# A new order of the units of the second attention, one store of rows a unit, and heads loaded from rows of sixteen

## The reference

```python
dist = softmax(mean(x @ Wr + br, axis=1))          # 16 heads, one row an image
idx = sort(top_k(dist, 4))                         # 4 heads of 16 for each image
Q, K, V = x @ Wq + bq, x @ Wk + bk, x @ Wv + bv    # 16 heads of 64 features
Qs, Ks, Vs = (the four chosen heads of each image)
O = softmax(Qs @ Ks.T / 8) @ Vs                    # 17 x 17 scores
return O.transpose(...) @ Wo + bo                  # then added to x
```

## Time and profile before

| what | value |
|---|---|
| runs | 406.89, 409.97, 404.96 us; median 406.89 |
| profiled execution | 407.69 us, its span 405.9 us |
| busy: PE, weight loads, DVE, ACT, POOL | 317.0, 259.3, 257.0, 202.8, 168.5 us |
| routing ready, first weights issued | 225.4 us from the span's start |
| first `qk` of unit 0, of unit 9 | 230.3 us, 348.8 us |
| last `head_out` begins with its pair at | 370.9 us |
| indirect fetch begins | 377.3 us |

### The profile page before, as it was taken

How to read it: one execution, slowest core, us unless ns; L and a number is a source line. 1 busy time by engine, 2 the same in 40 slices (tenths; PEclk the granted TensorE clock), 3 DMA queues, 4 the chain that set the end, 5 groups by cost and what they waited for, 6 DMA issues and landing times.

```text
span 405.9 us, 15412 instructions
## 1 busy us (share of the span) xinstructions
PE 317.0 (78%) x6584; PEld 259.3 (64%) x6584; DVE 257.0 (63%) x544; ACT 202.8 (50%) x461; POOL 168.5 (42%) x188
## 2 busy tenths in 40 slices
PE   1999999888877778758972598888796887672877
PEld 1896868346755656547852498777786876561366
DVE  2455555635778888875966477767775676633175
ACT  1113342637867666713891347666566565533140
POOL 3853000005366666630550733566644675352300
PEclk9999999999955555556985579999999999987699
DMA  7999100008000000000000678788686776722614
GB/s 205 390 427 405 81 2 0 0 0 289 26 3 6 5 4 5 3 5 2 2 1 0 203 228 266 232 247 242 173 267 170 231 224 177 225 69 48 199 62 184
DMA packets 40225, 53.84 MB, mean 133 GB/s; under 512 B 13244, under 2 KB 36956, under 8 KB 39644
## 3 DMA queue, kind: packets, MB, share of 16 engines
q1 hardware_dynamic: 39068, 50.50, 38.5%
q0 software_dynamic: 576, 2.23, 1.6%
q10 hardware_dynamic: 512, 0.11, 0.2%
HBM read 45.02 MB, written 7.81 MB: 130 GB/s over the span
## 4 chain that ended last, share of the span: by engine, by line
PE 34%; SPq 28%; DVE 12%; issue 11%; ACT 6%; DMA 4%; POOL 4%; POOLq 0%; ACTq 0%; DVEq 0%
SPq L433 17%; PE ps L1291 11%; SPq L422 5%; PE ps L1314 5%; SPq L438 5%; PE ps L1445 4%; POOL r L512 3%; DVE r L984 3%; PE ps L1627 3%; PE ps L1374 3%; PE ps L1396 2%; DVE rs L994 2%; PE ps L1329 2%; DMA r<-in_x 2%; DVE mx L969 2%
## 5 line engine op out<-in xcount | busy, mean ns | idle before, releaser
L505 POOL TENSOR_TENSOR r<-r,cst 128x1088 f32<-128x1088 f32 x16 | 33.0, 2066 | 61.7 <-DVE ring L920 58.9
L1291 PE MATMUL ps<-r 128*128 128x256 f32 x192 | 45.4, 392 | 8.7 <-DMA r<-in_x 8.7
L1291 PEld LDWEIGHTS ps<-r 128*128 128x128 f32 x192 | 37.4, 198 | 15.7 <-issue 10.6
L1396 PE MATMUL ps<-r 17*32 17x34 f32 x2048 | 30.3, 242 | 16.5 <-DVE r L984 11.8
L1396 PEld LDWEIGHTS ps<-r 17*32 17x32 f32 x2048 | 27.3, 142 | 24.3 <-DVE r L984 18.9
L697 ACT ACTIVATE r<-r,cst 128x136 f32<-128x136 f32 x128 | 39.9, 402 | 0.0
L1511 PE MATMUL ps<-r,ring 128*128 128x68 f16 x840 | 37.2, 201 | 1.9 <-issue 1.9
L767 ACT ACTIVATE r<-ps 128x504 f16<-128x504 f32 (+1 forms) x50 | 32.1, 667 | 11.4 <-PE ps L1489 10.8
L1489 PE MATMUL ps<-pairs_of,r 128*128 128x56 f16 x680 | 29.7, 193 | 9.7 <-DVE r L1156 5.8
L588 POOL TENSOR_TENSOR r<-r,quad 128x476 f16<-128x476 f16 x38 | 37.0, 1008 | 0.0
L1509 PE MATMUL ps<-tile_head,wb 128*128 128x68 f16 x140 | 27.8, 199 | 10.2 <-DMA ring<-wsplit 8.3
(11 more groups left out here) (160 smaller groups left out, 752.5 us busy)
## 6 DMA issues: line engine op xcount, KB each, us to landing
ring<-wsplit SPq DMA_DIRECT2D x140, 192.0 KB, 3.2
r<-in_x SPq DMA_DIRECT2D x3, 1536.0 KB, 15.8
r<-in_w SPq DMA_DIRECT2D x4, 768.0 KB, 12.7
wsplit<-ring SPq DMA_DIRECT2D x1, 3072.0 KB, 11.7
padded_rows<-r SPq DMA_DIRECT2D x36, 56.0 KB
r<-in_x SPq DMA_DIRECT2D x4, 384.0 KB, 8.7
h<-in_pos SPq DMA_DIRECT2D x1, 1536.0 KB, 11.9
out<-h SPq DMA_DIRECT2D x3, 512.0 KB, 2.7
```

Source lines behind the costliest of these rows:

```text
L505: pool.tensor_tensor(free(kx[:, u % 2, 0, :], (ROWH, UI), (NTOK, HH), (1, NTOK)), free(kr[:, 0, UI * NTOK * u:], (NTOK, UI), (0, HH), (1, ...
L1291: mm = pe.matmul(bank((n - 1) % 2, 0, D), xT[:, c, k, i * P:(i + 1) * P], tokw[:, k, :], start=k == 0, stop=k == PKT - 1)
L1396: mm = pe.matmul(bank(4 + 2 * (u % 2) + j // 2, at, at + 2 * NTOK)[QROW * c:QROW * c + QROW], v1[rows, UG * u + g, lo:lo + QROW], p1T[rows ...
```

## The change

Four things change together.

**Heads.** `heads` holds a row of 16 numbers for each unit, 14 of them used, so unit v's load begins at byte 64 v.

**Rows.** In `padded_rows` a pair has 32 rows of 256 bytes, not 17. One transfer stores all 128 partitions of a unit's `o2` (1,792 runs of 256 bytes, of which 840 are padding); the last unit has two such, by seven tiles, both on SP. ACT issues none. SP issues the weights of both parts of unit v and then the store of unit v - 3.

**Waits by part.** Where an instruction of part r of unit v waited until both parts of unit v - 2 were read, it waits for part r alone.

**Order.** All four engines get a new order. `weigh2` runs two units behind `qk`, not one, except at the end. `split_weights`, `low_halves` and `soft_out` are cut into their instructions, and these are placed one by one. The last unit has an order of its own on each engine. `gather`, `gathered`, `qk`, `v_of`, `scores2` and `weigh2` themselves are as before.

```diff
+HEADS_UNIT = 16
-PITCH = NTOK * HD2
+PITCH = QROW * HD2
...
-def pair_rows_of(v, j, lo=0, n=GU):
-    return bass.AP(padded_rows.tensor, (v * PU + IPG * lo + j) * PITCH,
...
+def rows_of(v, lo=0, n=GU):
+    return bass.AP(padded_rows.tensor, (v * PU + IPG * lo) * PITCH, [(HD2, P), (IPG * PITCH, n), (1, HD2)])
...
     def heads_of(v):
         _, head = nc.values_load_multi_w_load_instructions(
-            heads[0:1, GU * v:GU * v + GU], engines=(mybir.EngineType.SP,), min_val=0, max_val=NE - 1,
+            heads[0:1, HEADS_UNIT * v:HEADS_UNIT * v + GU], engines=(mybir.EngineType.SP,), min_val=0, max_val=NE - 1,
             skip_runtime_bounds_check_because="the head of a tile, and no more than NE - 1")
         return head
...
-    def store_pairs(v, j):
-        sp.dma_start(pair_rows_of(v, j), o2[QROW * j:QROW * j + NPATCH, v % 2])\
-            .then_inc(o2_stored[v % 2], 16)
-        if j == IPG - 1:
-            sp.dma_start(last_rows_of(v), o2[NPATCH:P:QROW, v % 2]).then_inc(o2_stored[v % 2], 16)
+    def store_rows(v):
+        sp.wait_ge(o2_ready, 2 * (v + 1))
+        sp.dma_start(rows_of(v), o2[:, v % 2]).then_inc(o2_stored[v % 2], 16)
     for v in range(NV):
         head = heads_of(v)
         weights_in(head, 2 * v)
+        weights_in(head, 2 * v + 1)
         if v >= 3:
-            sp.wait_ge(o2_ready, 2 * (v - 2))
-            for j in range(IPG):
-                store_pairs(v - 3, j)
-        weights_in(head, 2 * v + 1)
+            store_rows(v - 3)
     for v in range(NV - 3, NV - 1):
-        sp.wait_ge(o2_ready, 2 * (v + 1))
-        for j in range(IPG):
-            store_pairs(v, j)
-    last = o2[:, (NV - 1) % 2]
+        store_rows(v)
     for lo in (0, GR):
         sp.wait_ge(o2_ready, 2 * (NV - 1) + lo // GR + 1)
-        for j in range(IPG // 2):
-            sp.dma_start(pair_rows_of(NV - 1, j, lo, GR), last[QROW * j:QROW * j + NPATCH, lo:lo + GR])\
-                .then_inc(o2_stored[(NV - 1) % 2], 16)
-        sp.dma_start(last_rows_of(NV - 1, lo, GR), last[NPATCH:P:QROW, lo:lo + GR])\
+        sp.dma_start(rows_of(NV - 1, lo, GR), o2[:, (NV - 1) % 2, lo:lo + GR])\
             .then_inc(o2_stored[(NV - 1) % 2], 16)
...
         if v >= 2:
-            pool.wait_ge(s2_done, 2 * (v - 1))
-        if r == 0 and v == 0:
+            pool.wait_ge(s2_done, 2 * (v - 2) + r + 1)
+        if (v, r) == (0, 0):
             pool.wait_ge(xg_clear, 4)
             pool.wait_ge(bd_clear, 2)
-        elif r == 1 and v >= 1:
-            pool.wait_ge(bd_ready, 4 * v)
-        elif r == 0 and biased(v):
+        elif v <= 1 and (v, r) != (1, 1):
+            pool.wait_ge(k2_twice, 2 * v + r)
+        elif (v, r) == (NV - 1, 1):
+            pool.wait_ge(pT_high, NV - 1)
+        elif r == 1:
+            pool.wait_ge(bd_ready, 4 * (v - 1) + 1)
+        elif biased(v):
             pool.wait_ge(hbo_ready, biased(v))
         else:
-            pool.wait_ge(k2_twice, 2 * v + r)
+            pool.wait_ge(bd_ready, 4 * (v - 1))
...
-    def split_weights(v):
+    def split_high(v):
+        pool.wait_ge(k2_twice, min(2 * v + 3, 2 * NV))
         pool.wait_ge(p2T_ready, v + 1)
-        used = lambda x: free(p2Tx[:, v % 2, x], (QROW, GU), (1, NTOK))
-        full = free(p2T[:, v % 2], (QROW, GU), (1, NTOK))
...
-        pool.tensor_copy(used(0), full).then_inc(pT_high, 1)
+        pool.tensor_copy(free(p2Tx[:, v % 2, 0], (QROW, GU), (1, NTOK)),
+                         free(p2T[:, v % 2], (QROW, GU), (1, NTOK))).then_inc(pT_high, 1)
+    def split_low(v):
+        if v == NV - 2:
+            pool.wait_ge(k2_twice, 2 * NV)
         pool.wait_ge(pT_high, v + 1)
-        pool.tensor_tensor(used(1), full, used(0), ALU.subtract).then_inc(pT_low, 1)
...
     def block_diagonal(v, r, x):
-        if x:
-            pool.wait_ge(pT_low, v + 1)
-        elif v >= 2:
+        pool.wait_ge(pT_low if x else pT_high, v + 1)
+        if v >= 2:
             pool.wait_ge(pv2_done, 2 * (v - 2) + r + 1)
...
-    for v in range(NV + 1):
-        if v < NV:
-            keys_twice(v, 0)
+    keys_twice(0, 0)
+    for v in range(NV - 1):
         if v >= 1:
-            split_weights(v - 1)
-            for r in range(2 if v < NV else 1):
-                for x in range(2):
-                    block_diagonal(v - 1, r, x)
-        if v < NV:
-            keys_twice(v, 1)
-            if v >= 1:
-                pool.wait_ge(k2_twice, 2 * v + 2)
-            for n in range(biased(v), biased(v + 1)):
-                add_bias(n)
+            split_high(v - 1)
+            split_low(v - 1)
+            block_diagonal(v - 1, 0, 0)
+        keys_twice(v, 1)
+        if v >= 1:
+            pool.wait_ge(k2_twice, 2 * v + 2)
+            block_diagonal(v - 1, 0, 1)
+            block_diagonal(v - 1, 1, 0)
+            block_diagonal(v - 1, 1, 1)
+        for n in range(biased(v), biased(v + 1)):
+            add_bias(n)
+        keys_twice(v + 1, 0)
+    split_high(NV - 2)
+    keys_twice(NV - 1, 1)
+    split_low(NV - 2)
+    for r in range(2):
+        for x in range(2):
+            block_diagonal(NV - 2, r, x)
+    split_high(NV - 1)
+    split_low(NV - 1)
+    for x in range(2):
+        block_diagonal(NV - 1, 0, x)
+    for n in range(biased(NV - 1), NTOK):
+        add_bias(n)
     for i in range(2):
         pool.wait_ge(o2_stored[i], stores(i))
...
         if v >= 2:
-            act.wait_ge(pv2_done, 2 * (v - 1))
-            act.wait_ge(v2_low, 2 * (v - 1))
+            act.wait_ge(pv2_done, 2 * (v - 2) + r + 1)
+            act.wait_ge(v2_low, 2 * (v - 2) + r + 1)
...
-    for v in range(NV):
-        def next_fill(f):
-            if v + 1 < NV:
-                fill_out(v + 1, f)
+    for v in range(NV - 1):
+        fill_out(v + 1, 0)
         if v >= 1:
             pick(v - 1)
-        q_out(v, 0)
+        fill_out(v + 1, 2)
         k_high(v, 0)
-        next_fill(0)
         if v >= 1:
             exponent(v - 1)
+        q_out(v, 0)
         v_out(v, 0)
-        next_fill(2)
+        fill_out(v + 1, 4)
         q_out(v, 1)
         k_high(v, 1)
-        next_fill(4)
+        fill_out(v + 1, 6)
+        fill_out(v + 1, 7)
         v_out(v, 1)
-        next_fill(6)
-        next_fill(7)
+    pick(NV - 2)
+    k_high(NV - 1, 0)
+    exponent(NV - 2)
+    q_out(NV - 1, 0)
+    k_high(NV - 1, 1)
+    q_out(NV - 1, 1)
+    v_out(NV - 1, 0)
     pick(NV - 1)
     exponent(NV - 1)
+    v_out(NV - 1, 1)
     for x in range(2):
...
-    last = o2[:, (NV - 1) % 2]
-    for lo in (0, GR):
-        act.wait_ge(o2_ready, 2 * (NV - 1) + lo // GR + 1)
-        for j in range(IPG // 2, IPG):
-            act.dma_start(pair_rows_of(NV - 1, j, lo, GR), last[QROW * j:QROW * j + NPATCH, lo:lo + GR])\
-                .then_inc(o2_stored[(NV - 1) % 2], 16)
...
-    dve.tensor_copy(heads[0:1, :], bank(7, 64, 64 + NTILE)[0:1]).then_inc(heads_ready, 1)
+    dve.tensor_copy(free(heads[0:1, :], (HEADS_UNIT, NV), (1, GU)),
+                    free(bank(7, 64, 64 + NTILE)[0:1], (GU, NV), (1, GU))).then_inc(heads_ready, 1)
...
-    dve.tensor_scalar(idx[:, :], at_slot, float(NTOK), None, ALU.mult).then_inc(idx_ready, 1)
+    dve.tensor_scalar(idx[:, :], at_slot, float(QROW), None, ALU.mult).then_inc(idx_ready, 1)
...
-    def low_halves(v, r):
+    def q_low(v, r):
         dve.wait_ge(q2_ready, 2 * v + r + 1)
         if v >= 2:
-            dve.wait_ge(s2_done, 2 * (v - 1))
+            dve.wait_ge(s2_done, 2 * (v - 2) + r + 1)
...
+    def k_low(v, r):
         dve.wait_ge(k2_ready, 2 * v + r + 1)
+        if v >= 2:
+            dve.wait_ge(s2_done, 2 * (v - 2) + r + 1)
+        else:
+            dve.wait_ge(gap_clear, 2)
...
-    def soft_out(v):
+    def turn(v):
         dve.wait_ge(exp2_done, v + 1)
         if v < 2:
             dve.wait_ge(gap_clear, 3)
...
+    def total(v):
+        if v >= 2:
+            dve.wait_ge(rinv2_ready, v - 1)
         dve.tensor_reduce(rs[:, v % 2, 0:GU], p2[:, v % 2, :, 0:NTOK], AX_X, ALU.add).then_inc(rs2_ready, 1)
+    def inverse(v):
         dve.wait_ge(rs2_ready, v + 1)
         if v >= 2:
             dve.wait_ge(o2_ready, 2 * (v - 1))
...
-            dve.wait_ge(o2_stored[v % 2], v // 2 * (IPG + 1) * 16)
+            dve.wait_ge(o2_stored[v % 2], v // 2 * 16)
...
-    for v in range(NV):
-        def next_fill(f):
-            if v + 1 < NV:
-                fill_out(v + 1, f)
-        if v >= 1:
-            soft_in(v - 1)
-        low_halves(v, 0)
-        next_fill(1)
+    for v in range(NV - 1):
+        fill_out(v + 1, 1)
         if v == 0:
             one_hot(2 * PU, NPAIR)
         if v >= 1:
-            soft_out(v - 1)
+            soft_in(v - 1)
+        fill_out(v + 1, 3)
+        k_low(v, 0)
+        if v >= 1:
+            turn(v - 1)
+        fill_out(v + 1, 5)
         v_low(v, 0)
-        next_fill(3)
-        low_halves(v, 1)
-        next_fill(5)
+        q_low(v, 0)
+        q_low(v, 1)
+        k_low(v, 1)
+        if v >= 2:
+            head_out(v - 2, 1)
```

(66 more changed lines are left out.)

28 lines of the change are left out of this document (10 added, 18 removed).

## The result

The changed kernel takes 393.7 us (median of four runs, 391.6 to 395.0) against 407.4 for the kernel before in the same series: a ratio of 0.966, 95% interval 0.958 to 0.973. It is 3.4% faster, inside the range that was given, at the upper edge of the forecast's own 382 to 394, and 5.7 us above the number. The profiled execution took 391.6 us, with a span of 389.8.

A forecast was written before the change was run, and what follows sets the result against it. PE was taken to be bound by the order up to unit 7, then by SP, with DMA close behind. Terms summed to 19.6 us off the profiled 407.7, forecast 388 us; its own range 382 to 394, over all 382 to 399.

The forecast's parts named there:

- units 4 to 8: PE's 11.3 against DMA's 11.4 us: 12.0 a unit taken (bounds 11.2 and 13.2), 6.1 us gained.
- What bounds the kernel: PE bound by the order up to unit 7, then by SP, which needs about 12.6 us a unit.
- Heads: SP's ten head loads: all should take 1.2 us from 16-byte-aligned starts, 8.5 us off SP, hidden behind PE.
- Store issue: SP's queue: one transfer for five, 2.55 us to about 0.45 a unit (bounds 0.41 and 2.55).
- Store's packets: DMA queues: 1,792 packets cost 2.8 us a unit, so DMA needs 11.4 us a unit.
- rival 3: Stores beside weights: small packets cost double, DMA becomes the bound, store 5.7 us, time 402.7; chance 0.07.
- Order: PE's loop closes at 10 to 10.5 us; 11.3 taken for units 1 to 3, 3.7 us gained.
- Unit 0: First unit, at the low clock: two gathers and a shorter head load fill gaps, 0.5 us gained.
- Unit 9: Last unit: without weight waits, scores end after 6.7 us against 14.5; 0.5 charged for POOL's blocks; 7.3 us gained.
- Last store: From the last `head_out` to the fetch: about 3.1 us instead of 5.1, 2.0 us gained.
- Tail: Fetch to end: as many bytes read, only further apart, what follows unchanged; nothing gained or lost.
- rival 2: All nine units: the order gives nothing, only SP's relief does; PE stays at 12.5 us; time 395; chance 0.10.

The follow-up runs named there:

- again: The changed kernel measured once more without an edit: 393.1 us, ratio 0.967.
- the old-order runs: Kernel before with only head rows of 16: 402.8 us; with new head rows, single stores and SP's new order, other engines' order and waits old: 404.1 us.
- the reordered ones: Changed kernel with old head rows, five stores and SP's old order: 414.4 us; the same with the stores behind both parts' weights: 406.8 us.
- thin weights: Changed kernel with each weight transfer from the fourth part on cut to 16 of 128 partitions: 385.8 us, ratio 0.948.
- 34: Changed kernel with 34 idle matmuls instead of 24 between last store and output projection: 391.9 us, ratio 0.961.
- the run with SP's relief alone: Kernel before with new head rows, single stores and SP's new order, but old order and waits on the four other engines: 404.1 us, ratio 0.992.

## Why the prediction was right, and where it was not

The forecast's terms against the two profiled executions of the changed kernel, each against before (us gained; the terms sum to the difference of the spans, to 0.1):

| term | forecast | first | again |
|---|---|---|---|
| start of unit 0 | 0 | -0.3 | 0.1 |
| unit 0 | 0.5 | 2.8 | 2.9 |
| units 1 to 3 | 3.7 | 2.4 | 3.0 |
| units 4 to 8 | 6.1 | 10.3 | 5.6 |
| unit 9 to last `head_out` | 7.3 | 1.6 | 2.2 |
| last store to fetch | 2.0 | 1.1 | 1.1 |
| fetch to end | 0 | -1.9 | -2.0 |
| sum | 19.6 | 16.0 | 12.9 |

*What bounds the kernel*: right. SP and the old order, one just above the other; the old-order runs show 12.3 us a unit with SP out of the way, the reordered ones PE waiting for weights with SP in it. What the change leaves as the bound was wrong: "This part takes SP out of the way". SP's round is 11.9 and 12.3 us in the two executions, no shorter than PE's units 4 to 8 (11.1 and 12.1), and it never waits for `v_of`.

*Heads*: right in mechanism. All loads fall to 1.2 to 1.4 us where only their rows are moved. In the changed kernel those behind a store take up to 2.8, for a reason that is the store's. (The 10.2 us for a round with slow loads is a slip: 8.05 + 0.45 and a mean load of 2.03 make 10.5. Nothing hangs on it.)

*Store issue*: the instruction takes 0.42 us, but the term "0.45 on SP" was mis-sized, since what stands behind it is held for some 1.3 us more with thin weights. With full ones the six loads behind a store take 0.6 and 1.0 us more on the mean than those ahead of it, in the two executions. So it costs SP 1 to 1.7, inside the bounds of 0.41 and 2.55. With 14 weights at 8.5 instead of 8.05, SP's round measures 11.7 with thin weights where the forecast had 9.7; with full ones 14 weights take 8.6 to 10.7. SP is still the limit beside PE's 11.3.

*Store's packets*: 2.25 us a unit against 2.8, 20 ns a packet. Padding all the stores was cheap. The 512-byte rule of the Trainium skill ("DMA: Bandwidth & Descriptors", Specifications) does not decide here: writing the same bytes in runs above the limit saves some 0.8 of 2.25 us, less than half, and rival 3's 5.7 us a store did not appear.

*Order*: right for the floor (10.2 us, shown by the thin weights) and near it for what is reached with full ones (11.7 and 11.5 a unit for units 1 to 3, against 11.3). The new wait of `head_out` did no harm on DVE. "Unit 4 to unit 9 in 60 at a share above 0.9" was met by 60.5 at 0.90 in the second execution, and 55.7 at 0.91 in the first; the share could go above the 0.8 seen before.

*Unit 0*: mis-sized, 2.8 for 0.5. PE's clock was at its lower level up to 238.2 us; now it rises to 2.4 GHz at 229.3, falls back from 232.7 to 236.1 and stays up from there. PE is busy 10.0 us in the unit instead of 12.2, with as many matmuls, so about 2.2 of the 2.8 us are the clock. Of before, and then of after, stretches with the clock in the third column from the right:

```profile
234.00:238.00 4.00, 4.00 (x80) 4.00 (x78) 2.46 (x4) 1.79 (x3) 2.75 (x3) 0.50 0.47 159
```

```profile
230.00:232.00 2.00, 0.87 (x22) 0.73 (x21) 1.91 (x3) 0.99 (x2) 2.00 (x4) 1.00 0.93 306
234.00:238.00 4.00, 4.00 (x110) 4.00 (x108) 1.42 (x2) 2.23 (x4) 3.26 (x4) 0.73 0.85 287
```

Ahead of the rise PE runs five groups of 17 gathers in a row from 226.3 us, where it ran four and then waited 1.0 us for ACT and 1.3 for weights. The fifth group and the earlier rise go together in every trace of the new order that was read (first rise at 229.1 to 230.9 us, against 235.0 to 238.5 in the three of the old one); no run takes the group away, so the cause of the rise is not shown.

*Unit 9*: this step failed. "Without waits for weights, its scores end" 6.7 us after its start; they end 12.9 us after it. PE in the first part of unit 9:

```profile
335.22 0.20 PE L1542 MATMUL ps<-tile_head,wb 128*128 128x68 f16 x1 [0.85 <-DMA ring<-wsplit]
...
338.14 0.19 PE L1542 MATMUL ps<-tile_head,wb 128*128 128x68 f16 x1 [1.84 <-DMA ring<-wsplit]
...
340.06 0.24 PE L1542 MATMUL ps<-tile_head,wb 128*128 128x68 f16 x1 [0.84 <-DMA ring<-wsplit]
340.11 0.53 PE L1544 MATMUL ps<-r,ring 128*128 128x68 f16 x6
```

Three waits for weights in six us: SP's round is longer than PE's units, so PE had eaten SP's lead by then, and the last unit has no gathers for a next one that would fill the time. Then the price of a group of six matmuls goes from 0.36 to 0.53 us, as the clock falls:

```profile
338.50:345.00 6.50, 5.66 (x107) 5.50 (x103) 2.37 (x4) 1.15 (x2) 2.71 (x5) 0.50 0.37 90
```

5.66 us of matmuls at half the clock are some 2.8 lost. The 3.5 us of weight waits and this account for the 6.2 us between forecast and run. What follows the scores took 8.9 us before and after; the 0.5 charged for POOL's blocks did not appear. The new order makes it worse in one respect: `qk(9,1)` now stands ahead of `v_of(9,0)`, whose weights had long come, so everything waits for its weights (2.7 of the 3.5 us stand in `qk(9,1)`). That last point is argued from the order, not tried.

*Last store*: 1.1 gained for 2.0. The term's own parts, 0.45 + 1.4 + 2, make 3.85 us and not the 3.1 that was written; 4.0 were measured, so a gain of 1.3 would have been the forecast.

*Tail*: "what follows is unchanged: nothing" was wrong by 1.9 us. 1.4 of it is the clock behind too few idle matmuls: from ACT's first use of the fetched rows to the end it was 21.7 us before, is 23.1 now and 21.7 again with 34. The other 0.5 lies between the fetch's first issue and that use (6.8 us before, 7.3 now), and its cause stays open.

So the mechanism was the forecast's, with two steps wrong: SP out of the way, and unit 9 without waits. That the time still lies in the range is partly luck. In the first execution units 0 and 4 to 8 gave 6.5 us more than forecast and all else 10.1 less; in the second units 4 to 8 gave 5.6. The time is also close to rival 2's 395, by accident: its premise, that SP's relief does it all and the order gives nothing, is refuted by the run with SP's relief alone (0.992 against 0.966 with the order). Its "half of PE's waits have no named cause" was a third, 5.2 of 15.3 us in units 1 to 7.

## What to carry to other kernels

Where two limits lie within a few per cent, price the parts of a change by what each leaves as the next bound: here 0.8% and 0.1% alone made 3.4% together, and the new order with a wait in the old place made the kernel slower. Give an instruction on a queue the time until the next one runs, not its own duration. And cost the last pass of a loop by itself: nothing refills it, a wait there is not covered, and it can drop the clock for the work behind it.
